# A four-stage network on one core: pipelined front, split second norm, another order of side jobs in the first attention, a padded routing product, and feed-forward tokens transposed half a step later

## The chip, the core and the metric

One core of a Trainium2 chip runs the whole program. Its engines work side by side, each through its own list of instructions, and wait for each other on semaphores: TensorE (matrix products and transposes, PE in the profile; PEld is its weight load), VectorE (DVE), ScalarE (ACT), GpSimd (POOL), and SyncE (SP), which here issues all DMAs. The metric is the device time of one execution in microseconds, as the median of the runs.

## The reference

The input x has 16 sequences of 256 tokens of 128 features, in float32. In short:

```python
xn = layernorm(x)
s = window_attention(xn)            # 16 heads of 8, windows of 64, look back one window, distance bias
g = silu(experts(xn))               # router: softmax over 8, two best kept and renormalised; plus shared expert
x = x + s * g
xn = layernorm(x)
s = full_attention(xn)              # 16 heads of 8, 256 x 256, relative bias table, biases
g = silu(local_layers(xn))          # 2 layers: token shift, 8 heads of 64, windows of 64, rotary; gated feed-forward
x = x + s * g
```

In each inner layer the feed-forward part is: shift the tokens, norm them with gain and offset, multiply by w1 (128 to 2 x 341), value times gelu of the gate, multiply by w2, add to x.

## The kernel before

x, the normed tokens Y and the attention output S stay in SBUF as 32 tiles of 128 tokens. `build_kernel` (L81) runs these stages, each a block that all engines enter and leave together:

- `load_inputs` (L167): SyncE issues the relative bias, four quarters of X, the identity, the expert weights (3 MB), and a store of the extended bias to a scratch in DRAM. VectorE makes that extended bias first. The block ends when all of X, the identity and the store have landed.
- `layernorm` (L236), for `ln0` and again for `ln1`: VectorE takes statistics of 32 tiles (L254), then `moments` (L221) with `rsqrt` (L207, a bit trick and three Newton steps), then two passes over all of Y: subtract the mean (L257) and multiply (L259). In `ln1` SyncE loads the second attention's bias table (4 MB) at the same time (L117).
- `router` (L263): eight rounds of four tiles. GpSimd copies four tiles (L297), TensorE transposes them (L308), ScalarE keeps the transposed (L324), TensorE multiplies by the gate weights (L313), VectorE keeps the logits (L332). Then VectorE alone: softmax, a rank for each expert from 8 x 8 comparisons (L350 to L360), the two best kept (L362), and the weights as three bfloat16 parts (L374 to L379).
- `head_attention` (L383) with `windowed=True`. Work goes by units of 8 heads of one tile; a tile has two units, a batch four, and the lists of all engines are written out over steps, one unit a step. At a step with an even number TensorE makes the scores of units step+4 and step+5 (`score`, L550); at each step it transposes the probabilities (`transposes`, L571) and multiplies by the values (`sums`, L580). VectorE adds the bias (L700), takes the row maximum (L706) and divides (`normalise`, L708); GpSimd subtracts the maximum (L508); ScalarE takes exponentials (L667) and keeps the transposed probabilities (L672). Side jobs share PSUM bank 7: token transposes "x", Q and K "qk", values "v" (all ahead of the step's scores), and the output product "y" of one tile at the end of a step (L547). ScalarE empties the bank after each (L642 to L662), and the next job waits for that.
- `experts` (L748): eight rounds of 512 tokens, each 14 steps of 128 hidden features. A step has three split products for the gate, three for the up projection (L817 to L819), in the first 11 steps one that spreads the routing weights (L848, `sel16` with 24 rows, bfloat16), and three for the down projection of two steps ago. VectorE multiplies (L953, L957), ScalarE and GpSimd split the result in two parts (L919, L932). At step 2 VectorE updates X (L960, L963); at steps 8 and 10 the next round's tokens and routing weights are transposed.
- `head_attention` with `windowed=False`: the same for whole sequences with the loaded table. It loads its weights and biases at its start (L473 to L479).
- `inner_layers` (L982): 64 tiles (two layers of 32), one a step, and feed-forward rounds R of four tiles, spread over steps from 4R+5: staging by DMA at 4R+5, `moments` at +6, `deviations` (L1575) and `mlp_tokens` (L1292, the transposes) and `keep_mlp_tokens` (L1589) at +7, three `mlp_chunk` at +8 to +10, gelu and `gate` at +11, `mlp_out` at +12 and +13. TensorE's list in a step is: scores, Q and K projection, transposes of the output, of the probabilities, value projection, next tokens, output product, `mlp_out`, `sums`, transposes of Q and K, `mlp_chunk`, `mlp_tokens` (L1316 to L1357). VectorE's: `norms`, `square_sums`, `add_mask` (L1504), `sines`, `keep_token`, `add_out`, `add_mlp`, `quotient`, `deviations`, `keep_mlp_tokens`, `keep_value`, `moments` (L1609 to L1645). The value projection waits for `add_mask`, since scores and values share PSUM banks 2 and 3.
- `finish` (L1648): silu, product, sum and store of the result.

## Time and profile before

| | us |
|---|---|
| median of 3 runs | 1960.74 |
| lowest and highest | 1957.76, 1961.09 |
| the profiled execution, its time | 1958.84 |
| its span, first to last instruction | 1956.5 |
| TensorE busy | 1619.0 (83%) |
| VectorE busy | 1375.9 (70%) |
| ScalarE busy | 1183.4 (60%) |
| GpSimd busy | 1087.8 (56%) |
| mean granted TensorE clock | 0.943 of full speed |

The stages in that execution, from their first instructions: loads, norm and router 0 to 96.2; first attention 96.2 to 348.2; experts 348.2 to 678.9; second norm 678.9 to 700.8; second attention 700.8 to 1102.2; inner layers 1102.2 to about 1936; finish to 1956.5. The busy shares are means over stages with different limits, so each stage is read by itself: how busy each engine is in it, and where the order in time shows an engine waiting, for whom, and what that one was doing. A duration of a row is the instruction's own; the distance between the starts of two rows is what the pair costs.

### The profile page before, as it was taken

The numbers are of one execution on the slowest core, as the hardware profiler recorded it, in microseconds if no ns is written. First come the engines' busy times: TensorE is split into PE (matmuls) and PEld (weight loads), VectorE is DVE, ScalarE is ACT, GpSimd is POOL, SyncE is SP. The second block draws the span as 40 slices with busy tenths as digits, with TensorE's granted clock in tenths as the row PEclk, the third lists the DMA queues.
The fourth block names the chain that finished last, engine by engine and source line by source line (L and its number), as shares of the span: only waits on it lengthen the run. The fifth ranks groups of instructions, "written<-read, shape, count | busy, mean of one in ns | idle before, by whom it ended". The sixth has DMA issues, their size and how long they took to land. (4 is left out here: it accounts for less than half of the span.)

```text
span 1956.5 us, 47756 instructions
## 1 busy us (share of the span) xinstructions
PE 1619.0 (83%) x18705; PEld 1187.8 (61%) x18705; DVE 1375.9 (70%) x2187; ACT 1183.4 (60%) x1972; POOL 1087.8 (56%) x632
## 2 busy tenths in 40 slices
PE   0479999699999739999999668888888999888863
PEld 0346666466666527677777447666666777666742
DVE  4468887444554569999999588877777777777633
ACT  0147767444444327777777558777777777777742
POOL 0166665244444327777776677666666666666413
PEclk9999999899999959999999879999999998999986
DMA  3010000000000140000000001111111111111101
GB/s 104 2 48 3 3 3 3 14 13 7 6 7 6 29 133 2 2 2 2 3 2 2 10 15 32 23 23 23 23 24 24 23 23 23 23 26 24 23 21 43
DMA packets 52210, 40.16 MB, mean 21 GB/s; under 512 B 24408, under 2 KB 44028, under 8 KB 51876
## 3 DMA queue, kind: packets, MB, share of 16 engines
q1 hardware_dynamic: 52004, 37.28, 7.4%
q8 instruction: 145, 2.38, 0.5%
q14 instruction: 61, 0.50, 0.1%
HBM read 15.68 MB, written 2.13 MB: 9 GB/s over the span
## 5 line engine op out<-in xcount | busy, mean ns | idle before, releaser
L508 POOL TENSOR_TENSOR a_prob<-a_prob,a_top 128x1024 f32<-128x1024 f32 x192 | 359.7, 1894 | 133.1 <-DVE a_top L706 133.1
L700 DVE TENSOR_TENSOR a_prob<-ps,a_table 128x1024 f32<-128x1024 f32 x192 | 226.2, 1220 | 70.6 <-PE ps L562 47.8
L932 POOL TENSOR_TENSOR e_hh<-e_h,e_hh 128x512 fp32r<-128x512 f32 x112 | 144.2, 1290 | 195.4 <-ACT e_hh L919 193.7
L672 ACT ACTIVATE a_probT<-ps 128x1024 f32<-128x1024 f32 x192 | 196.5, 1023 | 90.0 <-PE ps L576 89.9
L706 DVE TENSOR_REDUCE a_top<-a_prob 128x4 f32<-128x1024 f32 (+1 forms) x192 | 225.2, 1215 | 8.7
L576 PEld LDWEIGHTS ps<-ident,a_prob 128*128 128x128 f32 x1536 | 168.0, 141 | 95.5 <-issue 60.1
L667 ACT ACTIVATE a_prob<-a_prob 128x1024 f32<-128x1024 f32 x192 | 202.7, 1056 | 33.0 <-POOL a_prob L508 33.0
L576 PE MATMUL ps<-ident,a_prob 128*128 128x128 f32 x1536 | 208.9, 279 | 7.8 <-ACT a_probT L672 2.9
L1170 POOL TENSOR_TENSOR i_qk<-i_qk,i_rn 128x1024 f32<-128x1024 f32 x64 | 123.3, 1927 | 117.7 <-DVE i_rn L1498 117.7
L1157 POOL TENSOR_TENSOR i_qk<-i_raw,i_rot 128x1024 f32<-128x1024 f32 x64 | 152.0, 2375 | 47.8 <-issue 42.6
L953 DVE TENSOR_TENSOR e_h<-ps,e_sg 128x512 f32<-128x512 f32 x112 | 77.4, 691 | 143.7 <-PE ps L819 118.3
L902 ACT ACTIVATE e_sg<-ps 128x512 f32<-128x512 f32 x112 | 66.9, 597 | 160.0 <-PE ps L819 160.0
L1412 ACT ACTIVATE i_prob<-i_prob,i_top 128x128 f32<-128x128 f32 x512 | 156.3, 394 | 9.8 <-DVE i_top L1507 8.0
L1160 POOL TENSOR_TENSOR i_qk<-i_qk,i_rt 128x1024 f32<-128x1024 f32 x64 | 151.3, 2365 | 19.4 <-DVE i_rt L1515 12.4
L602 PE MATMUL ps<-a_probT,a_V 128*32 128x64 f32 (+1 forms) x4096 | 159.5, 250 | 1.7 <-DVE a_oT L713 1.5
L1377 ACT ACTIVATE i_raw<-ps 128x1024 f32<-128x1024 f32 x64 | 65.6, 1025 | 154.5 <-PE ps L1216 154.4
L609 PE MATMUL ps<-a_probT,a_ones 128*32 128x128 f32 x3072 | 154.3, 273 | 0.0
L602 PEld LDWEIGHTS ps<-a_probT,a_V 128*32 128x32 f32 x4096 | 90.6, 109 | 33.7 <-issue 31.0
L501 POOL TENSOR_TENSOR a_kM<-a_kT,a_own 128x1024 f32<-128x1024 f32 x32 | 60.6, 1894 | 69.9 <-ACT a_kT L651 52.7
L817 PE MATMUL ps<-e_xT,e_wgu_hi 128*128 128x512 f32 x224 | 91.3, 408 | 4.7 <-DVE e_wd_lo L977 4.7
L1515 DVE TENSOR_TENSOR i_rt<-ps,i_rot 128x512 f32<-128x512 f32 x128 | 82.1, 683 | 15.1 <-ACT i_raw L1377 14.9
L1303 PE MATMUL ps<-i_mT,i_w 128*128 128x512 f32 (+1 forms) x192 | 90.6, 594 | 2.2 <-DVE i_A L1600 2.2
(213 smaller groups left out, 3830.9 us busy)
## 6 DMA issues: line engine op xcount, KB each, us to landing
i_V<-i_V SPq DMA_DIRECT2D x96, 130.0 KB, 2.3
a_table<-skew_scratch SPq DMA_DIRECT2D x2, 2048.0 KB, 12.9
X<-in_L_attn_x SPq DMA_DIRECT2D x4, 512.0 KB, 6.3
a_table<-in_c_l_table SPq DMA_DIRECT2D x1, 2048.0 KB, 8.1
e_xs<-Y SPq DMA_DIRECT2D x8, 256.0 KB, 2.3
i_ms<-Y SPq DMA_DIRECT2D x16, 128.0 KB
out_dram<-X SPq DMA_DIRECT2D x4, 512.0 KB, 3.3
i_ms<-Y SPq DMA_DIRECT2D x16, 127.0 KB
```

Source lines behind the costliest of these rows:

```text
L508: nc.gpsimd.tensor_tensor(s, s, top[:, slot].unsqueeze(2).broadcast_to([P, HG, KW]), ALU.subtract).then_inc(shifted, 1)
L576: last = nc.tensor.transpose(ps[:, 4 + b // 4, (b % 4) * P:(b % 4 + 1) * P], flat[:, b * P:(b + 1) * P], ident[:, :])
L602: nc.tensor.matmul(ps[32 * g:32 * g + 32, 6, cols], vals[:, 32 * x:32 * x + 32], src[:, at + cols.start:at + cols.stop], start=(first and ...
L609: last = nc.tensor.matmul(ps[32 * g:32 * g + 32, 6, P:2 * P], ones[:].rearrange("p x d -> p (x d)")[:, 32 * x:32 * x + 32], src[:, at:at + ...
L667: nc.scalar.activation(s, s, ACT.Exp).then_inc(exped, 1)
L672: nc.scalar.activation(probT[:, n % 4].rearrange("p (b n) -> p b n", b=2), ps[:, 4:6, :], ACT.Copy).then_inc(pT_sb, 1)
L700: nc.vector.tensor_tensor(prob[:, slot].rearrange("p (b x) k -> p b x k", b=2), ps[:, 2 * (n % 2):2 * (n % 2) + 2, :].rearrange("p b (x k) ...
L706: nc.vector.tensor_reduce(top[:, slot], prob[:, slot], AX.X, ALU.max).then_inc(max_done, 1)
L932: nc.gpsimd.tensor_tensor(hh[0:n, b % HBUF, 1, :], h[0:n, b % HBUF, :], hh[0:n, b % HBUF, 0, :].bitcast(F32), ALU.subtract).then_inc(h_lo, 1)
L1157: nc.gpsimd.tensor_tensor(s, raw[:, T % 2], cosines, ALU.mult).then_inc(cos_done, 1)
L1160: nc.gpsimd.tensor_tensor(s, s, rt[:], ALU.add).then_inc(rotated, 1)
L1412: last = nc.scalar.activation(s, s, ACT.Exp, bias=top[:, T % 2, h:h + 1])
```

## The change

1. `load_inputs`, the first `layernorm` and `router` become one block, `front`. Each quarter of X has its own semaphore, and statistics begin on the first. The inverse deviation comes from ScalarE (logarithm and exponential) with one Newton step on VectorE. Tiles are scaled one at a time, three of four on VectorE and one on ScalarE, and TensorE transposes round i from Y itself before it multiplies round i-1, with two buffers for the transposed tokens and no copy on GpSimd. The logits stay in PSUM. The two best experts are found as the first of the largest, twice, on 256 elements per partition, in place of 8 x 8 comparisons on 2048. The extended relative bias is made on GpSimd.
2. The second norm is split: VectorE takes the statistics of four tiles in each expert round, right after the update of X; the block `normalise` then makes the deviations as above and scales 16 tiles on ScalarE and 16 on VectorE.
3. In the first attention the scores come before the side jobs in TensorE's list, and the exponential before the side job in ScalarE's; the output products of a batch share the job of the token transposes four batches later ("xy"), with four buffers of `oT`.
4. `sel16`, the staged routing weights and their transposed form get 128 rows, the added ones zero, cleared by GpSimd at the stage's start.
5. In the inner layers `mlp_tokens` goes from the end of step 4R+7 to step 4R+8, ahead of `sums`; `keep_mlp_tokens` goes to step 4R+8, ahead of `quotient`. `deviations` stays.
6. `head_attention` is written out as two functions; the second attention's work and order stay the same.

```diff
+def front(nc, t, ps, X, Y, ident, wgu, wd, sel, experts_loaded, skew, wparts):
...
+            def transpose(i):
+                pe.wait_ge(own_rows, i + 1)
+                pe.wait_ge(other_rows, i + 1)
+                if i >= 2:
+                    pe.wait_ge(x_sb, i - 1)
+                for k in range(4):
+                    last = nc.tensor.transpose(ps[:, i % 2, k * P:(k + 1) * P], Y[:, 4 * i + k, :], ident[:, :])
+                last.then_inc(x_T, 1)
+            def multiply(i):
+                pe.wait_ge(x_sb, i + 1)
+                for k in range(4):
+                    at = (4 * i + k) * NE
+                    last = nc.tensor.matmul(ps[:, 2, at:at + NE], xT[:, i % 2, k * P:(k + 1) * P], gwT[:, :], start=True, stop=True)
+                last.then_inc(logits, 1)
...
+            for i in range(ROUNDS):
+                transpose(i)
+                if i:
+                    multiply(i - 1)
+            multiply(ROUNDS - 1)
...
+            for q in range(4):
+                dve.wait_ge(x_loaded[q], 16)
+                for k in range(QT):
+                    nc.vector.bn_stats(stats[:, QT * q + k, :], X[:, QT * q + k, :])
...
+            for i in range(ROUNDS):
+                for k in range(3):
+                    n = 4 * i + k
+                    last = nc.vector.tensor_scalar(Y[:, n, :], X[:, n, :], mean[:, n:n + 1], rstd[:, n:n + 1], ALU.subtract, ALU.mult)
+                last.then_inc(own_rows, 1)
...
+            def first_of_largest(dst, src):
+                nc.vector.tensor_reduce(st[:, :], src, AX.X, ALU.max)
+                dve.drain()
+                nc.vector.tensor_tensor(dst, src, bc(st), ALU.is_equal)
+                dve.drain()
+                nc.vector.tensor_tensor(dst, dst, order, ALU.mult)
+                dve.drain()
+                nc.vector.tensor_reduce(st[:, :], dst, AX.X, ALU.max)
+                dve.drain()
+                nc.vector.tensor_tensor(dst, order, bc(st), ALU.is_equal)
+                dve.drain()
...
+def normalise(nc, name, X, Y, stats, loads):
+            inverse_deviations(nc, act, rstd[:, :], var[:, :]).then_inc(seeded, 1)
+            act.wait_ge(refined, 1)
+            for n in range(0, NT, 2):
+                nc.scalar.activation(Y[:, n, :], X[:, n, :], ACT.Identity, bias=shift[:, n:n + 1], scale=rstd[:, n:n + 1])
...
+            for n in range(1, NT, 2):
+                nc.vector.tensor_scalar(Y[:, n, :], X[:, n, :], mean[:, n:n + 1], rstd[:, n:n + 1], ALU.subtract, ALU.mult)
...
+def window_attention(nc, name, t, ps, ident, Y, S):
+        AT = {'xy': -7, 'qk': -6, 'v': 0}
+        DELAY = 4
...
+                if kind == 'xy':
+                    if i < NBATCH:
+                        for k in range(TPB):
+                            last = nc.tensor.transpose(ps[:, 7, k * P:(k + 1) * P], Y[:, i * TPB + k, :], ident[:, :])
+                    if i >= DELAY:
+                        for k in range(TPB):
+                            T = (i - DELAY) * TPB + k
+                            pe.wait_ge(o_sb, T + 1)
+                            last = nc.tensor.matmul(ps[:, 7, (2 + k) * P:(3 + k) * P], oT[:, T % 4, :], wT[:, 3, :], start=True, stop=True)
...
+            for step in range(FIRST, LAST):
+                if step % 2 == 0 and 0 <= step + AHEAD < UNITS:
+                    score(step + AHEAD)
+                for n, kind, i in jobs_at(step):
+                    job(n, kind, i)
+                if 0 <= step < UNITS:
+                    transposes(step)
+                if 0 <= step - 2 < UNITS:
+                    sums((step - 2) // 2, step % 2)
...
-        sel16 = sb("sel16", [3 * NE, ROUTED], BF16)
+        sel16 = sb("sel16", [P, ROUTED], BF16)
-        ws = sb("ws", [P, 4, 3 * NE])
+        ws = sb("ws", [P, 4, P])
-        wT = sb("wT", [3 * NE, 2, N], BF16)
+        wT = sb("wT", [P, 2, N], BF16)
...
+                        for k in range(4):
+                            nc.vector.bn_stats(stats[:, bass.ds(i * 4 - 4 + k, 1), :], X[:, bass.ds(i * 4 - 4 + k, 1), :])
...
+                R, c = round_at(step, 8)
+                if R is not None and c == 0:
+                    projections_taken(pe, step)
+                    if not is_tile(step + LEAD):
+                        banks_01_free(pe, step)
+                    mlp_tokens(R)
                 if is_tile(step - 1):
                     sums(step - 1)
...
-                R, c = round_at(step, 7)
-                if R is not None and c == 0:
-                    projections_taken(pe, step)
-                    if not is_tile(step + LEAD):
-                        banks_01_free(pe, step)
-                    mlp_tokens(R)
...
+                R, c = round_at(step, 8)
+                if R is not None and c == 0:
+                    keep_mlp_tokens(R)
                 if is_tile(step - 1):
                     quotient(step - 1)
                 R, c = round_at(step, 7)
                 if R is not None and c == 0:
                     deviations(R)
-                    keep_mlp_tokens(R)
```

## Rows read from the trace of the kernel before

**Rows 1.** Busy time by stage: stretch, length, busy PE, PEld, DVE, ACT, POOL, clock, DMA.

```profile
96.20:348.20 252.00, 225.53 (x4388) 157.14 (x4388) 187.76 (x192) 164.16 (x274) 155.53 (x88) 0.99 0.04 12
348.20:678.90 330.70, 299.93 (x1192) 197.86 (x1192) 159.57 (x227) 146.54 (x253) 144.22 (x112) 0.97 0.02 8
678.90:700.80 21.90, 0.00 (x0) 0.00 (x0) 19.43 (x51) 0.00 (x0) 0.00 (x0) 0.50 0.66 192
1102.20:1936.00 833.80, 690.32 (x7168) 544.61 (x7168) 605.81 (x1242) 584.32 (x1107) 500.40 (x266) 0.92 0.10 22
```

**Rows 2.** Order in time, front: start, length, engine, line, what [idle before <- releaser].

```profile
21.00 1.94 DVE L254 BATCH_NORM_STATS2 ln_st<-X  x8 [17.96 <-PEq L170]
...
49.99 1.09 PE L308 MATMUL ps<-ident,r_xs 128*128 128x128 f32 x4
...
51.85 1.88 PE L313 MATMUL ps<-r_gwT,r_xT 128*128 128x8 f32 x8 [0.76 <-ACT r_xT L324]
...
75.40 0.19 DVE L332 COPY r_lg<-ps 128x32 f32 x1 [3.39 <-PE ps L313]
...
78.51 2.29 DVE L350 TENSOR_TENSOR r_gt<-r_lg 128x2048 f32<-128x2048 f32 x1
...
90.54 0.42 DVE L362 TENSOR_TENSOR r_wdense<-r_lg,r_rank 128x256 f32<-128x256 f32 x1
```

**Rows 3.** The four loads of X: issue times, and time from issue to landing.

```profile
L189 SPq DMA_DIRECT2D X<-in_L_attn_x x4: 409/1050/1578, 1.2 to 3.8; - x4
...
DMA to landing us min/median/max: 4.5/6.3/7.0
```

**Rows 4.** Order in time, one tile of the first attention.

```profile
201.61 0.49 PE L547 MATMUL ps<-a_wT,a_oT 128*128 128x128 f32 x2
...
202.46 1.16 PE L542 MATMUL ps<-a_wT,a_xT 128*128 128x128 f32 x8 [0.37 <-ACT S L662]
...
204.77 2.36 DVE L700 TENSOR_TENSOR a_prob<-ps,a_table 128x1024 f32<-128x1024 f32 x2 [1.22 <-PE ps L562]
...
208.90 0.49 PE L547 MATMUL ps<-a_wT,a_oT 128*128 128x128 f32 x2
```

**Rows 5.** Order in time, TensorE in the expert stage.

```profile
570.95 0.39 PE L848 MATMUL ps<-e_wT,e_sel 24*128 24x512 bf16 x1
...
572.08 0.40 PE L817 MATMUL ps<-e_xT,e_wgu_hi 128*128 128x512 f32 x1
572.31 0.39 PE L818 MATMUL ps<-e_xT,e_wgu_hi 128*128 128x512 f32 x1
...
573.55 0.39 PE L848 MATMUL ps<-e_wT,e_sel 24*128 24x512 bf16 x1
...
590.63 0.51 PE L817 MATMUL ps<-e_hh,e_wd_hi 128*128 128x512 f32 x1 [0.47 <-POOL e_hh L932]
```

**Rows 6.** The bias table: issue, issue to landing; VectorE's first step behind the biases.

```profile
678.92 2.21 SPq L117 DMA_DIRECT2D a_table<-skew_scratch  x2
...
DMA to landing us min/median/max: 9.8/12.9/16.0
...
708.46 0.15 DVE L692 TENSOR_SCALAR a_bqk<-a_bqk 128x1 f32<-128x1 f32 x1 [7.95 <-DMA a_bvo<-in_L_attn_bo]
```

**Rows 7.** Order in time, inner layers, where feed-forward tokens are transposed.

```profile
1501.73 1.09 PE L1233 MATMUL ps<-ident,i_qk 128*128 128x128 f32 x8
...
1505.77 1.11 DVE L1585 TENSOR_SCALAR i_G<-i_ms,i_mv,i_rstd 128x128 f32<-128x128 f32 x4
...
1507.04 0.99 PE L1295 MATMUL ps<-ident,i_G 128*128 128x128 f32 x4 [4.21 <-DVE i_G L1585]
...
1508.07 0.81 DVE L1593 TENSOR_SCALAR i_mT<-ps,i_vecs 128x512 f32<-128x512 f32 x1 [1.18 <-PE ps L1295]
...
1510.74 1.22 DVE L1504 TENSOR_TENSOR i_prob<-ps,i_mask 128x1024 f32<-128x1024 f32 x1
...
1512.90 0.48 PE L1222 MATMUL ps<-i_w_hi,i_h_hi 128*128 128x512 f32 x1
```

779 lines of the change are left out of this document (466 added, 313 removed).

## Prediction

> **What bounds the kernel now.** One core runs seven stages, one behind the other, each in a block of its own that ends for all engines together. So the chain that ended last is short and says little (it begins in the last 20 us); I read busy time by stage first [rows 1], then the order in time inside each stage that the change touches [rows 2 to 7]. The reader is to see three kinds of stage. The first attention (252.0 us) and the expert stage (330.7 us) keep TensorE busy for 225.5 and 299.9 us at a clock of 0.99 and 0.97: there only work or gaps of TensorE count. The second norm (21.9 us) is VectorE alone, busy 19.4 us, with TensorE at rest. The inner layers (833.8 us) have no full engine: TensorE is busy 690.3, VectorE 605.8, at a clock of 0.92, and the waits between the two set the end. The front, 0 to 96.2 us, is a serial chain: statistics from 21.00, router rounds, a ranking from 78.51 to 90.54 [rows 2].
>
> **Front (loads, norm, router).** (a) Statistics. Now they wait until 21.00 for the end of the loading block, which also holds a store for the bias table. After the change each quarter of X has a semaphore. The quarters are issued from 1.2 to 3.8 and land 4.5 to 7.0 us later [rows 3], so the first is there at 5.7 and the last by 10.8. Eight statistics cost 1.94 us [rows 2]; four such groups from 5.7 end at about 13.6. (b) The small chain behind them: some nine VectorE steps of about 0.19 us with drains, two ScalarE steps and two handovers, an estimate of 2.9 us; it ends at 16.5. (c) Rows are scaled at 0.28 us each (four take 1.11 us, [rows 7]), three of four on VectorE; the first transposes start at 17.3, as soon as four rows are there, instead of behind two passes over all of Y. (d) A router round now takes copy, transposes, copy and products in turn. In the new order TensorE alone sets it: 1.09 for four transposes and 1.88 for the logits [rows 2], 2.97 us. Bounds: all eight rounds at this pace, 17.3 + 23.8 = 41.1; all at half of it, if these rows were at 1.2 GHz and a TensorE without pauses gets 2.4, 17.3 + 11.9 = 29.2. I take 33, nearer the lower end, since eight transposes of the same size take those 1.09 us in the inner layers, where TensorE is seldom idle [rows 7]. (e) Behind the last logits there are now 96.2 - 75.4 = 20.8 us. The ranking with 2048 elements per partition (12.0 us, 78.51 to 90.54) becomes twelve operations on 256 elements, 0.42 us and a drain of 0.08 each [rows 2], 6.0 us; one copy goes: 14.6 us. The stage ends at 33 + 14.6 = 47.6 instead of 96.2. **Gain 48.6** (40.5 to 52.4).
>
> **First attention, other order.** Now each tile of 7.29 us (201.61 to 208.90) has TensorE do the output product alone, 0.49 us, then wait 0.37 us for ScalarE's copy of it, since one PSUM bank serves all side jobs [rows 4]; the scores come behind these jobs, and VectorE waits 1.22 us for them. After the change the scores go first and two tiles' output products share a job with the token transposes, four batches late. TensorE saves per batch twice (0.49 + 0.37) and pays one double product, about 0.5 us: 1.2 us. In 16 batches 19 us. What is next: VectorE needs about 6.07 us per tile (7.29 less 1.22), TensorE 7.29 - 0.6 = 6.69, so TensorE stays last and VectorE keeps a pause of 0.6. ScalarE's order (exponential, side job, kept transpose) costs nothing while the side job's copy lies beside eight transposes of TensorE. The products for Q and V no longer stand before a change of tile shape, worth perhaps 0.1 us each. **Gain 20.** Bounds: 8 if new stalls eat half; 1.22 x 32 = 39 if TensorE's intervals hold more slack than I see.
>
> **Padded routing product.** A step of the expert loop is 2.60 us (570.95 to 573.55), for ten products. Nine equal ones have a pitch of 0.23 [rows 5], 2.09 in all, so the tenth costs 0.51: 0.28 more than its like. It is the only one with 24 rows. With 128 rows it should cost 0.23. 11 routed steps in 8 rounds: 88 x 0.28 = 24.6 us, if nothing else is late. Something is: the chain VectorE, ScalarE, GpSimd already makes TensorE wait 0.47 us in one step [rows 5] and less in others, and these waits grow by what TensorE is sooner there; I take off 0.7 per round. The clearing of the padded tiles lies on GpSimd, idle while ScalarE and VectorE split the weights at the start of the stage; the wider weight load of the four transposes costs 0.05 per round. The second norm's statistics come in here: four per round, 0.24 each and register steps, 1.2 us of VectorE at the place where it has no pause; two steps later TensorE feels some 0.5. So 24.6 - 8 x 0.7 - 7 x 0.5 - 1.5 for the first steps of the rounds, which VectorE limits: **gain 14.** Bounds: -4 (shape not the cause, statistics paid) and 23.
> The Trainium skill has two rules here that disagree. "TensorEngine Tiling (Array Packing)", Key Properties, says that a change of tiling mode drains the engine; by it the 0.28 goes and the stage gains as above. "TensorE: Matmul & The Clock Gate", Why this matters for your kernels, says that one product with 32 rows takes as long as one with 128; by that alone padding brings nothing. The trace shows both: the 24-row product's own duration is that of the others (0.39), and the gap is around it, which is what the first rule says.
>
> **Second norm.** Now 21.9 us, nearly all VectorE [rows 1]: statistics, small steps, two passes over Y. After: statistics of the last round only, 1.2 (in the stage before); 0.4 to enter the block; small steps 3.1; 16 rows on each of two engines at 0.28, 4.5; 9.2 in all. The second attention could start 12.7 us sooner. But the bias table, 4 MB, is asked for at the stage's start, 678.92, and lands up to 16.0 us after issue, at about 695 [rows 6], and the attention's weights and biases follow it in the same queue. Now they are issued at 700.8, behind an idle queue, and VectorE goes on with the biases at 708.46. After the change the table lands 17 us behind the stage's start while the weights are issued 8 us behind it; small loads end some 3 to 4 us behind the table. **Gain 9** (7 to 12.7). The Trainium skill, "DMA: Bandwidth & Descriptors", Queues, rings and completion order, says that descriptors of a ring are consumed in ring order; by it 9, without it 12.7.
>
> **Inner feed-forward tokens half a step later.** Once in four tiles TensorE, free at 1502.83, waits 4.21 us for VectorE's normalised tokens [rows 7]. VectorE in turn waits 1.18 for the transposes and spends 0.81 on keeping them before it can mask the next scores. After the change TensorE goes on with the next scores and projections, and VectorE from its last token (1506.88) straight to the mask. What is late next is that mask: it ends 5.1 us behind 1506.88 now, 3.0 after, and the value projection, now at 1512.90, 1 us after the mask, waits for it: it comes at about 1510.0, 2.9 us sooner. Then the step pays back: four transposes 0.43, and the first chunk waits about 0.4 for the kept tokens, which now come behind VectorE's token and output work. Net 2.0 us in 15 of 16 rounds (the last has nothing beside it), **gain 29**. Bounds: 10, if ScalarE or GpSimd is late behind them, and 45; the whole 4.2 us per round can't be had while VectorE's 3.0 stand.
>
> **Sum.** 48.6 + 20 + 14 + 9 + 29 = 120.6 us. The profiled execution took 1958.84 us (span 1956.5 and 2.3 around it), 0.1% under the median of 1960.74; 1960.7 - 120.6 = 1840. The second attention and the finish are as before.
>
> **Rivals.**
> Waits, not work, in the first attention: each tile gives back VectorE's whole 1.22 us. For it: the wait repeats in every tile. Against: TensorE busy 225.5 of 252.0. 1960.7 - 139.6 = 1821.
> The routing product keeps its gap: its cause would be the change of type (bf16 among 32-bit products), not of height, so the change doesn't do what it says; the skill's rule on rows would have it so too. For it: no row shows a full-height bf16 product. Against: that product itself is no longer than its neighbours (0.39 us), so its type costs nothing while it runs [rows 5]. 1840 + 18 = 1858.
> The inner wait comes back elsewhere, at the projection or the chunk. For it: three engines without a pause of their own set this loop. Against: VectorE really drops 2.1 us from its way to the mask. 1840 + 29 = 1869.
> Slower than before: the clock of the first attention. If the order with scores first left TensorE pauses that drop the clock from 2.4 to 1.2 GHz, its 6.69 us per tile would double, 214 us in 32 tiles, and the time be 1840 + 214 = 2054. It decides from 120 us on, that is when over 56% of the stage runs low. Against it: a granted clock of 0.99 now [rows 1], and the new order has fewer pauses.
>
> **Chances.** As forecast 0.58; whole wait in the first attention 0.12; gap stays 0.14; inner wait comes back 0.13; slow clock 0.02; nothing gained 0.01. Two of the middle ones together end near 1887. The terms' own bounds (front 8, attention 12 to 19, routing 9 to 18, norm 3, inner 16 to 19), taken as independent, make about 30 us to either side: 1806 to 1876. Measured changes below 0.2%, 4 us, count as the same. Faster 0.96, same 0.01, slower 0.03.
>
> **What would show it.** Right: the first attention starts near 48 us, lasts about 232, with VectorE's wait for scores at 0.6 or less; the expert steps take 2.32 us with all starts 0.23 apart; the second attention's first weight transposes come some 17 to 18 us behind the norm's start, ended by a DMA; the wait before the token transposes is gone, and one before the value projection has come in its place, some 2 us per round. Wrong: router rounds of 3 us to the end; a pause around the routing product; the time of the inner layers within 5 us of 833.8; more than 240 us in the first attention.

## The result and the profile after

The changed kernel takes 1850.26 us (median of 4 runs, 1846.08 to 1856.7), the kernel before beside it on the same chip 1960.91. The ratio is 0.944, with a 95% interval of 0.941 to 0.947: 110.7 us less, where 120.6 were forecast, and the forecast of 1840 is 10 us too low. The profiled execution took 1846.08 us, with a span of 1844.3.

Busy time by stage, with the columns of [rows 1]; the blocks are the front, the first attention, the experts, the second norm, the second attention, the inner layers and the finish:

```profile
0.00:50.23 50.23, 20.32 (x97) 19.92 (x97) 26.09 (x97) 10.15 (x22) 1.05 (x8) 1.00 0.37 101
50.23:285.04 234.81, 215.46 (x4388) 156.72 (x4388) 189.11 (x192) 162.02 (x258) 155.11 (x88) 1.00 0.04 13
285.04:599.86 314.82, 282.55 (x1176) 201.02 (x1192) 165.73 (x259) 149.02 (x254) 145.76 (x114) 0.96 0.03 8
599.86:609.31 9.45, 0.00 (x0) 0.00 (x0) 5.89 (x27) 8.00 (x19) 0.00 (x0) 0.50 0.86 255
609.31:1013.49 404.18, 380.14 (x5860) 268.54 (x5860) 352.66 (x385) 276.47 (x323) 271.37 (x150) 0.96 0.05 16
1013.49:1824.07 810.58, 681.23 (x7168) 533.98 (x7168) 603.52 (x1242) 585.91 (x1107) 499.88 (x266) 0.94 0.10 23
```

The clock column prints 1.00 where the trace holds no record of the clock, and its first record is at 79.33 us (114.51 in the kernel before). So the 1.00 of the front is not measured; the part on why the prediction was right comes back to it.

The reader is to see that the stages still stand one behind the other, so each term of the forecast has a length of its own to be held against. Beside [rows 1], with 401.3 us for the second attention before:

| stage | before | after | gain | forecast |
|---|---|---|---|---|
| front | 96.2 | 50.2 | 46.0 | 48.6 |
| first attention | 252.0 | 234.8 | 17.2 | 20 |
| experts | 330.7 | 314.8 | 15.9 | 14 |
| second norm and second attention | 423.3 | 413.6 | 9.6 | 9 |
| inner layers | 833.8 | 810.6 | 23.2 | 29 |
| sum | | | 111.9 | 120.6 |

The spans differ by 112.2; the finish has the remaining 0.3.

**Front.** Order in time, as in [rows 2]:

```profile
4.95 3.43 DVE L336 BATCH_NORM_STATS2 r_stats<-X 128x6 f32<-128x128 f32 x16 [4.95 <-DMA X<-in_L_attn_x]
8.55 3.41 DVE L336 BATCH_NORM_STATS2 r_stats<-X 128x6 f32<-128x128 f32 x16 [0.18 <-DMA X<-in_L_attn_x]
...
15.68 1.94 PE L269 MATMUL ps<-ident,Y 128*128 128x128 f32 x8 [4.40 <-DVE Y L344]
...
28.99 1.09 PE L269 MATMUL ps<-ident,Y 128*128 128x128 f32 x4
...
31.44 1.09 PE L269 MATMUL ps<-ident,Y 128*128 128x128 f32 x4
...
35.79 0.42 DVE L349 TENSOR_REDUCE r_st<-ps 128x32 f32<-128x256 f32 x1 [14.82 <-PE ps L276]
```

Statistics end at 11.96, transposes start at 15.68, and the rounds then come 2.45 us apart (28.99, 31.44), all eight of them, with TensorE busy throughout: 20.1 us up to the last logits at 35.79. Behind them the chain on VectorE takes 14.4 us, to the stage's end at 50.23; forecast was 14.6.

**First attention.** VectorE's bias additions in two tiles that follow each other, and its wait in the second (compare [rows 4]):

```profile
160.54 2.35 DVE L667 TENSOR_TENSOR a_prob<-ps,a_table 128x1024 f32<-128x1024 f32 x2 [0.21 <-issue]
...
166.77 2.36 DVE L667 TENSOR_TENSOR a_prob<-ps,a_table 128x1024 f32<-128x1024 f32 x2 [0.21 <-issue]
...
171.95 0.96 DVE L675 RECIPROCAL a_rden<-ps 128x128 f32<-128x128 f32 x1 [0.39 <-PE ps L599]
```

VectorE's wait for scores, 1.22 us per tile before, is gone. By these starts and the next, at 173.49, tiles of 6.23 and 6.72 us take turns, 12.95 per batch of two where it was 14.50. In the short tile VectorE has no pause left and is itself the limit; in the long one it waits 0.39 us for TensorE's sums.

**Second norm.**

```profile
599.85 2.28 SPq L115 DMA_DIRECT2D a_table<-skew_scratch  x2
...
617.04 1.11 PE L809 MATMUL ps<-ident,a_wnat 128*128 128x128 f32 x4 [19.91 <-DMA a_wnat<-in_L_attn_Wo]
```

The first weight transposes of the second attention come 17.2 us behind the norm's start and wait for a DMA, 7.7 us behind their own stage's start. The stage itself is 2.8 us longer than before, which is what the norm's 12.4 us of shortening pay back.

**Inner layers.** Groups of TensorE's instructions by line (busy time and mean of one, then the idle time in front of them and what ended it), and one round in order of time, beside [rows 7]:

```profile
L1464 PE MATMUL ps<-i_w_hi,i_h_hi 128*128 128x512 f32 x64 | 31.6, 493 | 46.0 <-DVE i_prob L1746 45.9
L1545 PE MATMUL ps<-i_mT,i_w 128*128 128x512 f32 (+1 forms) x192 | 93.3, 609 | 9.0 <-DVE i_mT L1835 6.8 <-DVE i_A L1842 2.2
L1537 PE MATMUL ps<-ident,i_G 128*128 128x128 f32 x64 | 10.3, 286 | 1.2 <-DVE i_G L1827 0.7 <-DVE i_rt L1757 0.5
```

```profile
1453.02 2.37 POOL L1402 TENSOR_TENSOR i_qk<-i_qk,i_rt 128x1024 f32<-128x1024 f32 x1 [0.16 <-issue]
...
1453.36 2.04 DVE L1820 SCALAR_TENSOR_TENSOR i_mtmp<-i_var,i_rstd 128x4 f32<-128x4 f32 x1
...
1455.97 1.11 DVE L1827 TENSOR_SCALAR i_G<-i_ms,i_mv,i_rstd 128x128 f32<-128x128 f32 x4
...
1458.95 1.21 DVE L1746 TENSOR_TENSOR i_prob<-ps,i_mask 128x1024 f32<-128x1024 f32 x1
...
1460.21 0.50 PE L1464 MATMUL ps<-i_w_hi,i_h_hi 128*128 128x512 f32 x1 [2.38 <-DVE i_prob L1746]
...
1462.29 2.77 PE L1554 MATMUL ps<-i_w,i_A 128*128 128x128 f32 x12
```

The wait in front of the token transposes fell from 64.6 us in all to 1.2. In its place the value projection (L1464) waits 45.9 us for the mask addition, 18.8 before; with smaller ones in front of the first chunk (9.0, was 2.2), the scores (12.9, was 5.4) and the output half (15.7, was 8.2). So 63.4 went and 48.9 came; TensorE's own busy time fell by 9.1 (690.3 to 681.2), with a mean clock of 0.94 instead of 0.92. 63.4 - 48.9 + 9.1 = 23.6, for 23.2 measured.

### The profile page after: what moved, and what is told of

Its sections match the earlier page's. It is cut to its first block and busy times, and to the rows that moved or that the text cites. A ratio compares the mean times of both kernels' runs of the same rounds, so it can differ in the third digit from the quotient of the medians.

```text
span 1844.3 us, 47459 instructions
## 1 busy us (share of the span) xinstructions
PE 1579.7 (86%) x18689; PEld 1180.2 (64%) x18705; DVE 1354.0 (73%) x2206; ACT 1196.7 (65%) x1985; POOL 1084.4 (59%) x629
## 3 DMA queue, kind: packets, MB, share of 16 engines
q8 instruction: 146, 2.39, 0.6%
## 5 line engine op out<-in xcount | busy, mean ns | idle before, releaser
L924 ACT ACTIVATE a_probT<-ps 128x1024 f32<-128x1024 f32 x128 | 131.0, 1023 | 72.0 <-PE ps L853 72.0
L1399 POOL TENSOR_TENSOR i_qk<-i_raw,i_rot 128x1024 f32<-128x1024 f32 x64 | 151.9, 2373 | 28.9 <-issue 23.6
L949 DVE TENSOR_REDUCE a_top<-a_prob 128x4 f32<-128x1024 f32 x128 | 150.1, 1215 | 5.8
L919 ACT ACTIVATE a_prob<-a_prob 128x1024 f32<-128x1024 f32 x128 | 134.8, 1053 | 29.1 <-POOL a_prob L797 29.1
L853 PEld LDWEIGHTS ps<-ident,a_prob 128*128 128x128 f32 x1024 | 111.7, 141 | 62.0 <-issue 35.8
L853 PE MATMUL ps<-ident,a_prob 128*128 128x128 f32 x1024 | 139.1, 279 | 4.6 <-ACT a_probT L924 1.2
L873 PE MATMUL ps<-a_probT,a_V 128*32 128x128 f32 x2048 | 105.9, 279 | 0.9 <-DVE a_oT L956 0.7
L877 PE MATMUL ps<-a_probT,a_ones 128*32 128x128 f32 x2048 | 102.8, 273 | 0.0
```

What stands on the lines that cost most here:

```text
L853: last = nc.tensor.transpose(ps[:, 4 + b // 4, b % 4 * P:(b % 4 + 1) * P], flat[:, b * P:(b + 1) * P], ident[:, :])
L919: nc.scalar.activation(s, s, ACT.Exp).then_inc(exped, 1)
L924: nc.scalar.activation(probT[:, n % 4].rearrange('p (b n) -> p b n', b=2), ps[:, 4:6, :], ACT.Copy).then_inc(pT_sb, 1)
L949: nc.vector.tensor_reduce(top[:, slot], prob[:, slot], AX.X, ALU.max).then_inc(max_done, 1)
L1399: nc.gpsimd.tensor_tensor(s, raw[:, T % 2], cosines, ALU.mult).then_inc(cos_done, 1)
```

## Experiments: which part brought what

Each kernel is the changed one with the edit shown. Where the code of a stage is the same, its length still differs between the profiles: 311.6 to 315.6 us for the experts, 233.5 to 235.0 for the first attention, 403.3 to 405.3 for the second, 810.6 to 820.3 for the inner layers (more on these below). A difference smaller than that is not told from nothing.

### The token transposes back in step 7

```diff
-                R, c = round_at(step, 8)          # TensorE, ahead of sums()
+                R, c = round_at(step, 7)          # TensorE, behind mlp_chunk()
                 if R is not None and c == 0:
                     ...
                     mlp_tokens(R)
-    keep_mlp_tokens(R) at round_at(step, 8), c == 0, ahead of quotient()
+    keep_mlp_tokens(R) behind deviations(R), and banks_01_free() waits for it again
```

> The changed kernel with one part undone: the four transposes of the feed-forward tokens and their copy stand in step 7 again, the rest stays. Theory (the wait for the normalised tokens is what the part removed): the inner layers go from 810.6 back to 833 to 835 us, TensorE waits about 4.2 us in front of the token transposes in most rounds (65 us in all), a low-clock stretch follows it once per round, and the time is 1850 + 23 = 1873. Rival (the stage gained for another reason, the clock or the order of the rest): inner layers 810 to 820, time under 1860.

1865.38 us, ratio to the kernel before 0.952 (0.950 to 0.955); the inner layers take 829.9 us.

```profile
L1467 PE MATMUL ps<-i_w_hi,i_h_hi 128*128 128x512 f32 x64 | 31.4, 491 | 18.7 <-DVE i_prob L1749 18.6
L1540 PE MATMUL ps<-ident,i_G 128*128 128x128 f32 x64 | 16.5, 409 | 49.8 <-DVE i_G L1830 49.8
```

The wait before the transposes is back and the one before the value projection is at its old 18.6, so the move trades one for the other, and the rival falls. The stage stays under the 833 to 835 us expected, and this wait is 49.8 us instead of 64.6, though both kernels have the same order of work here: in the kernel before, the first small step of the normalisation takes 2.04 us in nine of its 16 rounds, here 0.92 to 1.05 in the twelve in which it is long. The experiments on this step, below, say why. The low clock comes more often than expected: each of the twelve rounds has two stretches at a granted 0.50, one a step ahead of the wait and one at its end.

### The routing product over 24 rows again

```diff
-nc.tensor.matmul(ps[:, 4 + s % 2, :], sel16[:, a:a + n], wT[:, parity, :], ...)
+nc.tensor.matmul(ps[:, 4 + s % 2, :], sel16[0:24, a:a + n], wT[0:24, parity, :], ...)
```

> The changed kernel with the routing product taken over 24 rows of both operands again; the cleared buffers, the full-height transposes of the routing weights and the row statistics in the expert stage stay. Theory (the short product opens a pause behind itself, and the statistics cost a little in this stage): steps with a routing product go from 2.32 to 2.60 us, the expert stage from 314.8 to 332 to 336 us, above the 330.7 of before by what the statistics cost; time 1868 to 1871. Rival (the pause has another source, so height does nothing): the stage stays within 313 to 318 and the time near 1850. Second rival (statistics cost nothing): exactly 330.7.

1869.62 us, ratio 0.955 (0.953 to 0.957); the expert stage takes 332.4 us. So the padding brought 17.6 us against the changed kernel's own profile (16.8 to 20.8 against all eleven with the padded product), for 17.5 forecast, and the rival falls. The row statistics that came into this stage would have cost 332.4 - 330.7 = 1.7, for 3.5 forecast; but that is less than the 4.0 us by which the stage differs between profiles of the same code, so the second rival, that they cost nothing, is not refuted.

### One height for each chunk

```diff
+rows = (24, 24, 32, 32, 64, 64, 96, 96, 128, 128, 128)[s]
+nc.tensor.matmul(ps[:, 4 + s % 2, :], sel16[0:rows, a:a + n], wT[0:rows, parity, :], ...)
```

> The changed kernel with the routing product of the 11 chunks of a round over 24, 24, 32, 32, 64, 64, 96, 96, 128, 128 and 128 rows (the rows left out hold zeros, so the sum is the same). Read is the time from the start of the routing product to the start of the next product of another kind, 0.23 us at 128 rows and about 0.5 at 24. Theory 1 (the array changes to a smaller tile for up to 64 rows): 24, 32 and 64 rows 0.5 us, 96 and 128 rows 0.23. Theory 2 (anything below full height pauses): only 128 rows 0.23. Theory 3 (only heights that are no multiple of 32 pause): only 24 rows 0.5.

1860.27 us in its one run, the expert stage 324.6. TensorE in order of time, in one round:

```profile
417.07 0.40 PE L1059 MATMUL ps<-e_xT,e_wgu_lo 128*128 128x512 f32 x1
417.40 0.38 PE L1089 MATMUL ps<-e_wT,e_sel 24*128 24x512 bf16 x1
417.72 0.50 PE L1057 MATMUL ps<-e_xT,e_wgu_hi 128*128 128x512 f32 x1
...
429.05 0.40 PE L1059 MATMUL ps<-e_xT,e_wgu_lo 128*128 128x512 f32 x1
429.38 0.39 PE L1089 MATMUL ps<-e_wT,e_sel 64*128 64x512 bf16 x1
429.70 0.50 PE L1057 MATMUL ps<-e_hh,e_wd_hi 128*128 128x512 f32 x1
...
431.67 0.40 PE L1059 MATMUL ps<-e_xT,e_wgu_lo 128*128 128x512 f32 x1
431.90 0.39 PE L1089 MATMUL ps<-e_wT,e_sel 96*128 96x512 bf16 x1
431.94 0.59 PE L1057 MATMUL ps<-e_hh,e_wd_hi 128*128 128x512 f32 x1
```

The start behind a 96-row product is drawn early and its length late, so the sure measure is from the start of the product before to the second start behind: 0.98 us at 24, 32 and 64 rows (0.97 to 0.99 in 39 of 48 cases), and 0.70 at 96 (all 16) as in the commonest case at 128 (0.69 to 0.70 in 37 of the 72 on record in the changed kernel). Seven of the others are all the third product of a round, with 0.81 us at 32 rows and 0.57 to 0.58 at 128. The pause is 0.28 us, lies on both sides of the product (0.09 to 0.10 ahead, the same behind it and behind the next), and does not come from the type: the 96-row product is bf16 too. Theory 1 holds. By the Trainium skill, "TensorEngine Tiling (Array Packing)", Key Properties, a change of mode drains the engine, and its Available Configurations have tiles of 32 and 64 rows and none between 64 and 128; the runs agree with both.

### Scores of the first attention behind the side job

```diff
-    score(step + AHEAD)  # first in the step
     for n, kind, i in jobs_at(step):
         job(n, kind, i)
+    score(step + AHEAD)
```

> The changed kernel with TensorE's scores of the first attention behind the side job of the step again; the shared output product of two tiles and its delay stay. Theory (TensorE is the last engine, and the gain of 17 us is the output products and the wait for their copy that it no longer has): the first attention stays at 235 to 238 us, time 1850 to 1854. Rival (VectorE got its scores earlier, and that was the gain): VectorE's wait of 1.2 us for scores comes back in each tile, the stage goes to 246 to 252 us, time 1862 to 1867. A result between says how much each is.

1852.49 us, ratio 0.946 (0.943 to 0.948); the first attention takes 236.0 us, 1.2 more. The rival falls. The order of scores and side jobs is worth 0.30 us in each steady batch (13.25 us instead of 12.95), and most of that is given back at the start of the stage, as told below. The other 1.25 us per batch (14.50 - 13.25) are what the forecast priced at 1.2: the output product of two tiles in one job, and the wait for its copy that TensorE no longer has. ScalarE's new order stands in both kernels, and no run takes it by itself.

## Experiments: what limits the kernel now

### The second attention's small loads ahead of the bias table

```diff
 def normalise's sync block:
+    nine loads: Wq, Wk, Wv, Wo, own, bq, bk, bv, bo of the second attention
     load_bias_table(sp, skew, table, table_loaded)
 def bias_attention's sync block:
-    the same nine loads
```

> The changed kernel with the weights and biases of the second attention (nine small loads) issued in the stage of the second norm, ahead of the two 2 MB loads of its bias table in the same queue, instead of behind them. Theory (the 4 MB of the table hold the small loads back): the first weight transposes of the second attention come 2 to 4 us behind its start instead of 7.7, and it takes 5 to 7 us less than 404.2, if the table still lands by the first bias addition; time 1844. Rival (the first bias addition needs the table and the inner weights' loads crowd the start): the stage takes 0 to 2 us less.

1848.75 us, ratio 0.944 (0.942 to 0.945). The second attention takes 398.1 us, 6.1 less.

```profile
606.21 1.08 PE L819 MATMUL ps<-ident,a_wnat 128*128 128x128 f32 x4 [12.22 <-PEq L391]
...
609.00 0.60 ACT L906 ACTIVATE a_wT<-ps 128x512 f32<-128x512 f32 x1 [1.55 <-POOL a_ones L795]
```

The stage starts at 606.16 and its transposes 0.05 us later; behind them it is GpSimd's clearing that ends last, not a load. What the norm's stage seemed to lose, 2.8 us, was the queue, and 3.3 us more can be had. In the total the gain is hidden: this kernel's inner layers took 820.3 us.

### The ranking in two parts

```diff
+def rank_part(half, lo, hi): the chain from the maximum to wparts, on tiles lo to hi
+rank_part(0, 0, 12)      # waits for logits >= 3
+rank_part(1, 12, NT)     # waits for logits >= ROUNDS; its logits in another PSUM bank
```

> The changed kernel with the router's ranking in two parts, tiles 0 to 11 as soon as their logits are there (VectorE then waits 14.8 us for the last logits) and tiles 12 to 31 behind the last logits; each instruction of a part costs 0.15 us and 0.001 us per element, by 0.18 us for 32 and 0.42 for 256 elements. Theory (the tail of 14.4 us is VectorE's chain over all tiles): the tail falls to 10.5 to 11.5 us, the front from 50.2 to 46 to 47.5, time 3 to 4 us less. Rival (TensorE's rounds slow down, since ScalarE's exponential for the first part stands between its copies): rounds of over 2.45 us and a front of 49 to 52 us.

1851.63 us, ratio 0.945 (0.943 to 0.946); the front takes 48.05 us, 2.2 less, and the tail behind the last logits 12.2 instead of 14.4.

```profile
35.89 0.33 DVE L355 TENSOR_REDUCE r_st<-ps 128x20 f32<-128x160 f32 x1 [1.01 <-PE ps L276]
```

The first part runs from 24.37 us on, beside the rounds. The theory holds in direction, and TensorE's rounds are not disturbed (last logits 35.89 instead of 35.79), but the gain is 2.2 and not 3 to 4: a step on 160 elements costs 0.33 us and 0.07 between steps against 0.42 and 0.07 on 256, over most of 30 steps. I had overrated what falls away with size.

### The normalisation of the tokens later

The wait of 45.9 us for the mask addition stands behind VectorE's normalisation of the feed-forward tokens. Two kernels move that work behind the sines.

```diff
                     sines(step + LEAD)
+                R, c = round_at(step, 8)
+                if R is not None and c == 0:
+                    deviations(R)
...
-                R, c = round_at(step, 7)
-                if R is not None and c == 0:
-                    deviations(R)
```

> The changed kernel with one more move in the inner layers: VectorE normalises the feed-forward tokens (four small steps and four products, 2.6 us per round) behind the sines of step 8 instead of at the end of step 7, where they stand ahead of the next mask addition. Theory (the wait of TensorE for the mask addition, 45.9 us in the changed kernel, is what the work that VectorE does before it costs): that wait falls by 1 to 1.7 us in each of 16 rounds, the inner layers go from 810.6 to 788 to 798, time 1828 to 1838. Rival (the token transposes or the kept tokens come late instead, since they now follow directly): a wait of 1.5 to 2.5 us returns in front of the token transposes and the inner layers stay within 806 to 818, time near 1850.

> As the run before, and the moments of the feed-forward tokens (1.9 us per round) also stand behind the sines, of the same step 6, instead of at its end. Theory: the second, shorter wait of each round for the mask addition (0.8 us) goes too, the inner layers take 8 to 14 us less than with the deviations alone moved. Rival (the kept token transposes, now 1.9 us later, hold the value projection back): no gain over the run before, or up to 10 us more.

They take 1911.1 us (ratio 0.975) and 1928.55 us (0.984), with inner layers of 875.4 and 896.0 us: 65 and 85 us lost where 12 or more were to be gained, and far more than the rivals had (818 us at most, and up to 10 more). One round of the first:

```profile
1391.07 2.36 POOL L1402 TENSOR_TENSOR i_qk<-i_qk,i_rt 128x1024 f32<-128x1024 f32 x1 [0.62 <-DVE i_rt L1757]
1391.28 2.16 DVE L1824 SCALAR_TENSOR_TENSOR i_rstd<-i_mtmp,i_rstd 128x4 f32<-128x4 f32 x1
1393.38 1.90 POOL L1412 TENSOR_TENSOR i_qk<-i_qk,i_rn 128x1024 f32<-128x1024 f32 x1
1393.52 2.61 DVE L1827 TENSOR_SCALAR i_G<-i_ms,i_mv,i_rstd 128x128 f32<-128x128 f32 x4
...
1396.28 1.09 PE L1537 MATMUL ps<-ident,i_G 128*128 128x128 f32 x4 [4.52 <-DVE i_G L1827]
```

A step on four elements, 0.16 us when alone, begins 0.21 us behind the start of an instruction of GpSimd and ends within 0.02 us of its end. The four products behind it take 2.61 us instead of 1.11: the first, 0.34 us when alone, takes 1.84 and ends 0.08 behind GpSimd's next instruction, in each of 13 rounds. So the new place is bad in two ways: it comes late for the transposes, and it lies beside GpSimd's rotation, where the whole chain takes 5.3 us instead of 2.6 to 3.7. The mask addition's wait did fall, to 25.2 us, and the transposes' rose to 61.8. Waits are not all of it: of the 65 us, 28 are TensorE's own busy time, 709.4 us instead of 681.2, at a mean clock of 0.90 instead of 0.94.

### The same steps in another form

Was it the form of these instructions that waits? Three kernels write the chain with tensor_tensor alone.

```diff
-nc.vector.scalar_tensor_tensor(mtmp[:], var[:], -0.5, rstd[:], ALU.mult, ALU.mult)
+nc.vector.tensor_tensor(mtmp[:], var[:], rstd[:], ALU.mult)      # var holds -0.5 (var + eps)
...
+nc.vector.tensor_tensor(mn[:], ms[:], mv[:, :, 0:1].broadcast_to([P, 4, P]), ALU.subtract)
+nc.vector.tensor_tensor(mtmp[:], mtmp[:], half3[:], ALU.add)
+nc.vector.tensor_tensor(rstd[:], mtmp[:], rstd[:], ALU.mult)
+nc.vector.tensor_tensor(mn[:], mn[:], rstd[:, :].unsqueeze(2).broadcast_to([P, 4, P]), ALU.mult)
```

> The changed kernel with the normalisation of the feed-forward tokens, in its place at the end of step 7, written in another kind of instruction: the first scalar_tensor_tensor (0.15 us alone, 1.35 on the mean, 2.05 where GpSimd is in a tensor_tensor, and then it ends within 0.03 us of GpSimd's instruction), the second one and the four tensor_scalar (1.12 us) become six tensor_tensor. Theory (these forms wait for GpSimd, a tensor_tensor does not, by its 0.16 us in the middle of a GpSimd instruction): no instruction of the new chain is longer than its size asks, the chain takes about 2.2 us in every round in place of 2.9 to 3.7, TensorE's wait for the mask addition behind it falls by 0.7 to 1.4 us a round, and the inner layers take 8 to 18 us less than 810.6 to 820. Rival (GpSimd's use of memory slows every form): the first instruction still takes 1 to 2 us and the stage stays at 810 to 820.

> The same rewriting in the kernel whose normalisation stands behind the sines of step 8, whose inner layers took 875.4 us (token transposes waiting 4.52 us a round). Theory (that move was dear because each of its instructions ran into GpSimd's and waited for them, 5.2 us for a chain of 2.2): the wait falls to 1.2 to 2 us, and the inner layers to 820 to 840. Rival (the place alone makes it late): the wait stays over 3 us and the stage over 855.

> The same rewriting with the token transposes back in step 7, where the inner layers took 829.9 us and the transposes waited 49.8 us in all. Theory (of the wait that the change removed, 0.8 to 1.9 us of 4.2 per round were VectorE waiting for GpSimd in front of the normalised tokens): the wait falls to 2 to 3.3 us a round and the stage to 812 to 822, so that much of what the move of the transposes brought could be had without it. Rival (the wait is the chain's own length): 826 to 834.

The theory of the form falls in all three. The rival of the later place holds as written; the other two kernels are slower still than their rivals had it (810 to 820 and 826 to 834 us). In place the kernel takes 1859.12 us (ratio 0.949, inner layers 824.9 us), in the later place 1908.53 (0.975, 872.2), with the transposes back 1879.19 (0.959, 848.2). One round of the second:

```profile
1389.12 0.16 DVE L1824 TENSOR_TENSOR i_mtmp<-i_mtmp,i_rstd 128x4 f32<-128x4 f32 x1
1389.14 2.36 POOL L1403 TENSOR_TENSOR i_qk<-i_qk,i_rt 128x1024 f32<-128x1024 f32 x1 [0.62 <-DVE i_rt L1759]
1389.36 2.69 DVE L1826 TENSOR_TENSOR i_G<-i_ms,i_mv 128x512 f32<-128x512 f32 x1
1391.46 2.34 POOL L1413 TENSOR_TENSOR i_qk<-i_qk,i_rn 128x1024 f32<-128x1024 f32 x1
1391.97 1.85 DVE L1827 TENSOR_TENSOR i_mtmp<-i_mtmp,i_half 128x4 f32<-128x4 f32 x1
```

A tensor_tensor from SBUF waits too (L1827, four elements, 1.85 us, to within 0.02 us of GpSimd's end), and while VectorE works off its part (L1826 to 1392.05), GpSimd's next instruction takes 2.34 us instead of 1.90. My evidence against it had been a row of 0.16 us "in the middle" of a GpSimd instruction; these rows show that it began 0.02 us ahead of that instruction. So the two engines exclude each other one instruction at a time when VectorE reads two operands from SBUF. The tensor_scalar products above, with one tensor and two columns of scalars from SBUF, wait as well. It is not so when one operand comes from PSUM, or for a reduction: the mask addition (PSUM and SBUF, 1.22 us) and the row maximum (L1749, 1.22 us) have the same length beside GpSimd and without it. Nor is it so beside GpSimd's clearing at the start of the stage: there steps with two SBUF operands keep their 0.18 to 0.23 us. The Trainium skill, "SBUF — State Buffer", "SBUF: two separate sides", has the rule: the port pair that VectorE and GpSimd share is locked for a whole instruction, and on VectorE's side operations in a two-port mode ask for it, or with two SBUF inputs against an instruction of GpSimd that reads SBUF. The rows agree; that the tensor_scalar products run in a two-port mode no row shows.

The tensor_tensor chain is also longer when undisturbed (2.23 us against 1.82), since its two 128x512 passes cost 0.69 each. These 0.41 us in 16 rounds are 6.6 of the 8.9 us by which the kernel in place is slower than the changed one; the rest is not explained.

### Two gains together

```diff
+ the nine small loads ahead of the bias table, and the ranking in two parts, as above
```

> The changed kernel with the two additions that each shortened a stage: the second attention's nine small loads ahead of its bias table (stage 398.1 in place of 404.2 us) and the router's ranking in two parts (front 48.05 in place of 50.2). Theory (stages stand one behind the other, so gains of different stages add): 6.1 + 2.2 = 8.3 us under the changed kernel's 1850.3, 1842, give or take what the inner layers scatter between runs (810.6 to 820.3 us). Rival (the gain of one is lost in another stage): 1847 or more.

1845.08 us (5 runs), ratio 0.943 (0.941 to 0.944), beside 0.944 (0.941 to 0.947) for the changed kernel: the intervals overlap, so the total does not prove a gain. By stage it is there: front 48.4 and second attention 399.2 us, 1.9 and 5.0 less. The inner layers took 817.2 us in that profile, and their scatter covers it. The rival is not needed: no stage got longer through the edits, but the total cannot exclude it either.

## Why the prediction was right, and where it was off

**Front, 46.0 for 48.6.** Two errors half cancel. The statistics ended 1.6 us sooner than worked out, since the first quarter was there at 4.95 and eight statistics cost 1.71 us instead of 1.94 (they are written out now; before they stood in a loop). The router rounds were mis-sized: I took 33 for their end, and it was 35.8. The step that failed is that a TensorE without pauses would get 2.4 GHz during the rounds. It got none of it:

```profile
20.00:25.00 5.00, 5.00 (x27) 5.00 (x26) 0.96 (x4) 1.95 (x4) 0.00 (x0) 1.00 0.00 0
...
77.61 1.88 PE L575 MATMUL ps<-ident,a_prob 128*128 128x128 f32 x8
...
80.61 1.09 PE L575 MATMUL ps<-ident,a_prob 128*128 128x128 f32 x8 [0.90 <-ACT a_probT L648]
...
289.60:291.00 1.40, 1.12 (x4) 0.72 (x4) 0.00 (x0) 1.40 (x2) 0.00 (x0) 0.50 0.00 0
...
430.96 0.60 PE L1065 MATMUL ps<-ident,e_xs 128*128 128x128 f32 x4
```

The 1.00 in the first line is printed without a record behind it, so the pace of equal products has to tell the clock. Four transposes of 128x128 take 1.09 us in the front (at 28.99, above). Four of the same size (L1065) take 1.12 us in the expert stage at 289.69, where the recorded clock is 0.50, and 0.60 at 430.96, where it is 1.00. So the front ran at 1.2 GHz from its first transposes to its last logits, though TensorE had no gap in it. The pace doubles only in the first attention, from the eight transposes at 77.61 to those at 80.61, and there, at 79.33, the record of the clock begins with 1.00. The guess that the rows of 1.09 and 1.88 us were at 1.2 GHz was right, and the row that was to speak against it, eight transposes in 1.09 us in the inner layers, says the same: half of the pace. So the upper bound's case, this pace to the end, is what happened, only with rounds of 2.45 us and not 2.97: the logits took 1.71 us and the seams overlap by 0.2 and 0.15. The mark "router rounds of 3 us to the end" came true in kind. The tail was right.

**First attention, 17.2 for 20.** The steady state is better than forecast: 1.55 us per batch, of which 1.25 are the output products, priced at 1.2, and 0.30 the order of scores, priced at nothing. The rival that VectorE's wait was the prize is refuted by the order's 1.2 us in the whole stage. What was mis-sized is the number of batches, 16: the gain shows in 13 of them (20.7 us). The start and the end of the stage got longer:

```profile
71.81 1.89 POOL L506 TENSOR_TENSOR a_kM<-a_kT,a_own 128x1024 f32<-128x1024 f32 x1 [1.29 <-ACT a_kT L631]
...
73.81 2.01 PE L567 MATMUL ps<-a_kM,a_qT 32*64 32x512 f32 x16 [2.49 <-POOL a_kM L506]
```

The third scores of the stage wait for the second batch's keys, which now come behind the scores in TensorE's order: from first to third scores 11.0 us here, 9.7 before and in the kernel with late scores. From the third to the fourth it is 7.8 us, 6.8 before, and the low clock goes with it: in four kernels with the same order, in which the record of the clock begins 20 to 21 us behind the start of the stage instead of 29, it is 6.8 again. The last tile takes 0.9 us more. From the first bias addition to the last scores 197.4 us pass, 17.7 less than before. "TensorE stays last" holds for every second tile only.

**Routing product, 15.9 for 14.** Right in mechanism and, by the 24-row run, in the size of the padding: 17.6 (17.5 forecast). The size of the statistics, 1.7 for 3.5, is within the scatter. The pause is 0.28 as read, and as forecast it can't be had everywhere: around the sixth and the tenth product of most rounds TensorE waits, and the three starts there take 1.03 to 1.15 us (0.97 with 24 rows) and 1.20 to 1.22 (1.22 with 24 rows).

**Second norm, 9.6 for 9.** The queue did hold the small loads back, 17.2 us behind the norm's start where 17 to 18 was said, and taking them out of it gave back 6.1 us. The block itself took 9.5 us, where 8.0 were left of the 9.2 without the statistics counted in the stage before; the queue set the end, so this cost nothing.

**Inner tokens, 23.2 for 29.** Steady rounds fell from 47.95 to 46.2 us, 1.75 for the 2.0 forecast, and the next late step was the mask, as named. VectorE's way was read rightly: from the last normalised token to the end of the mask 3.08 us in all 13 steady rounds (3.0 forecast), and in rounds like the one read the value projection starts 6.85 us behind the small step instead of 9.72, 2.87 sooner (2.9). Two things were mis-sized. The first is what such a round pays back, 2.87 - 1.75 = 1.12 us where 0.83 were taken off; which of its steps has the 0.3 more was not settled. With it goes a wait that the forecast took as it stood: the small step in front of the tokens takes 0.15, 0.9 to 1.3, or 2.05 us, by how much of a GpSimd instruction lies ahead of it. Its long rows were in the trace of before, and I did not ask what they waited for. In the changed kernel eight rounds with 2.05 us give TensorE a wait of 2.36 to 2.39, four with 0.93 to 1.33 one of 1.72 to 1.77.

The second is the clock, which the forecast left out for this stage. In the round shown above, L1554 takes 2.77 us for twelve products; in others 1.50. The clock in that stretch, and in one without such a slow part:

```profile
1448.00:1468.00 20.00, 15.58 (x170) 13.35 (x170) 15.84 (x33) 14.65 (x33) 15.68 (x8) 0.91 0.10 22
...
1352.00:1372.00 20.00, 15.08 (x166) 12.63 (x166) 17.02 (x36) 16.91 (x34) 14.40 (x8) 1.00 0.07 15
```

In the kernel before, each of the nine waits of 4.2 us, and three of the four of 2.7 (not the one that ends at 1222), have at their end, or from inside them on, a stretch of 3.4 us (in three of the twelve 6.8) at a granted clock of 0.50 (1.2 GHz). In the changed one three of the eight waits of 2.4 us have it (at 1181, 1460 and 1600), and such a round is 1.5 to 1.7 us longer than its like: the second and third take 47.7 and 47.9 instead of 46.2, and the first is in the opening round, which takes 46.15 us in three kernels with the stretch there and 44.5 in four without it there. Four other stretches of the changed kernel lie a step earlier, behind two waits of 0.8 and 0.9 us (as at 1403.5 to 1407), and their rounds lose nothing by it: they are the four in which VectorE's small step meets only 0.93 to 1.33 us of GpSimd's instruction, as everything comes a little later. How many long rounds there are differs from kernel to kernel with nothing changed in this stage: 2 of 47.7 to 48.2 us with a stage of 810.6 in the changed kernel, 4 with 814.1 in the 24-row one, 5 with 814.0 in the one with late scores, 7 with 818.0 in the one with the ranking in parts. So 810.6 is the lowest of its kind: against the one profile of before, the seven profiles with this code (810.6 to 820.3 us) give gains of 23.2 down to 13.5, and that the first came near the forecast is in part luck. What decides whether a wait of 2.4 us lowers the clock was not settled.

Of the rivals, the gap of the routing product and the return of the inner wait came out false as wholes, though three quarters of that wait did return as others (48.9 of 63.4 us); the slow clock of the first attention did not occur beyond its start (1.00 on record from 79.33 us on).

## What to carry to other kernels

Before moving a small VectorE step, look at what GpSimd does at the new place, and at how many operands the step takes from SBUF: here the same four-element step cost 0.16 or 2.16 us, and a move meant to save 12 to 23 us lost 65. A product with 24 to 64 rows among full-height ones costs its own time and 0.28 us more, so zeros up to the full height are cheaper than the short form. When a wait of TensorE is removed, price the next late engine by all its rows and not by one round, and add what the clock gives back if the wait was followed by a stretch at 1.2 GHz. Before taking a printed clock of 1.00 at face value, compare the pace of equal products in a stretch whose clock is on record.

## What the runs showed of the hardware that was not expected

- The array's change of height costs 0.28 us at 24, 32 and 64 rows and nothing at 96.
- In the front TensorE was busy from 15.68 to 35.8 us without a gap and stayed at 1.2 GHz throughout: its transposes take 1.09 us for four, as at a recorded 0.50. The pace doubled only at 79.3 us, 29 us into the first attention.
- VectorE and GpSimd wait for each other's whole instruction when VectorE reads two operands from SBUF: 2.16 us for a step of 0.16; GpSimd's instruction of 1.90 us became 2.34. A tensor_scalar with one SBUF tensor waits too (1.84 us for 0.34), a reduction does not.
- Stretches of 3.4 us at 1.2 GHz inside a loop in which TensorE is busy 84% of the time: at all nine waits of 4.2 us and three of four of 2.7 in the kernel before, at three of eight waits of 2.4 us in the changed one. Behind the mask's wait each costs some 1.6 us of a round of 46.2; a step earlier it costs nothing.
